# Two halves of one result side by side: where VectorE's list has the first norm's sum in the third quarter of a band

## What is computed

```python
def _arsinh_norm(x, w, b):
    return w * jnp.arcsinh(x) + b
...
    qkv = x @ qkv_w + qkv_b
    q, kk, v = jnp.split(qkv, 3, axis=-1)
...
    scores = jnp.einsum('bijnd,bijmnd->bijnm', q, nb_k)
    attn = jax.nn.softmax(scores, axis=-1)
    out = jnp.einsum('bijnm,bijmnd->bijnd', attn, nb_v).reshape(B, H, W, C)
    return out @ proj_w + proj_b
...
h1 = _arsinh_norm(h, n1_w, n1_b)
h = h + _na2d(h1, qkv_w, qkv_b, proj_w, proj_b)
h2 = _arsinh_norm(h, n2_w, n2_b)
ff = jax.nn.gelu(h2 @ mlp_w1 + mlp_b1, approximate=False) @ mlp_w2 + mlp_b2
return h + ff
```

## Time and profile before

| what | value |
|---|---|
| median of 3 runs | 4478.32 us (4474.22 to 4479.34) |
| the profiled execution's own time | 4478.71 us |
| its span | 4476.9 us |
| busy share: TensorE, VectorE, ScalarE, GpSimd | 91%, 80%, 82%, 79% |
| granted clock of TensorE, share of full speed | 0.97 |
| chain that ended last: TensorE, VectorE, issue, ScalarE | 51%, 23%, 14%, 10% |

### The profile page before, as it was taken

The page is one execution under the profiler, slowest core; times in us unless marked ns, Lnnn a source line. Parts: engine busy times, 40 slices in busy tenths (PEclk is TensorE's granted clock), DMA queues, the critical chain, the costliest instruction groups (busy, mean ns, idle before and its releaser), DMA issues.

```text
span 4476.9 us, 123492 instructions
## 1 busy us (share of the span) xinstructions
PE 4089.1 (91%) x47688; PEld 2566.3 (57%) x47688; DVE 3570.1 (80%) x6174; ACT 3663.0 (82%) x5377; POOL 3539.3 (79%) x4092
## 2 busy tenths in 40 slices
PE   5999999999999999999999999999999999999997
PEld 3555555555555555555555555555555555555553
DVE  5788788888878888887888888788878888887884
ACT  4888888888888888888888888888888888888884
POOL 2788888887888888888878888888888788788885
PEclk8999999999999999999999999999999999999998
DMA  4555555555555555555555555555555555555551
GB/s 121 129 142 134 136 135 138 138 134 137 138 135 134 141 137 132 142 134 138 133 140 138 133 136 139 136 133 142 133 137 135 138 138 133 137 138 136 134 133 55
DMA packets 511560, 598.82 MB, mean 134 GB/s; under 512 B 76798, under 2 KB 409600, under 8 KB 508416
## 3 DMA queue, kind: packets, MB, share of 16 engines
q1 hardware_dynamic: 510976, 590.93, 51.2%
HBM read 197.30 MB, written 135.40 MB: 74 GB/s over the span
## 4 chain that ended last, share of the span: by engine, by line
PE 51%; DVE 23%; issue 14%; ACT 10%; POOL 1%; SPq 1%; DMA 0%; DVEq 0%; POOLq 0%; ACTq 0%
PE ps L369 49%; DVE ln_u L717 4%; DVE y L790 4%; DVE v_nat L771 4%; DVE o_norm L812 3%; DVE ln_u L713 3%; ACT ln_s L920 3%; ACT ln_s L911 3%; ACT ln_s L915 3%; DVE ln_u L710 2%; ACT q_nat L944 2%; PE ps L446 2%; DVE maxima L796 2%; DVE recip L803 1%; POOL g_lo L1098 0%
## 5 line engine op out<-in xcount | busy, mean ns | idle before, releaser
L1072 POOL TENSOR_TENSOR p_lo<-prob,p_hi 100x512 f16<-100x512 f32 x1024 | 1312.7, 1287 | 623.7 <-ACT p_hi L990 623.5
L369 PE MATMUL ps<-b_hi,w_hi 128*128 128x512 f16 x1024 | 435.7, 425 | 288.4 <-DVE y L790 283.3
L989 ACT ACTIVATE prob<-ps 100x512 f32<-100x512 f32 x1024 | 610.2, 596 | 80.2 <-PE ps L369 54.9
L713 DVE TENSOR_TENSOR ln_u<-ln_u,ln_s 128x1024 f32<-128x1024 f32 x256 | 531.0, 2074 | 147.2 <-ACT ln_s L920 143.4
L812 DVE TENSOR_TENSOR o_norm<-ps,recip 64x128 f32<-64x128 f32 x2048 | 591.7, 289 | 49.4
L1098 POOL TENSOR_TENSOR g_lo<-g,g_hi 128x512 f16<-128x512 f32 x512 | 594.9, 1162 | 41.0
L369 PEld LDWEIGHTS ps<-v_win,p_hi 100*128 100x128 f16 x8192 | 474.7, 98 | 261.3 <-DVE o_norm L812 70.7
L990 ACT ACTIVATE p_hi<-ps 100x512 f16<-100x512 f32 x1024 | 613.7, 599 | 0.0
L796 DVE TENSOR_REDUCE maxima<-ps 128x8 bf16<-128x800 f32 x512 | 504.6, 986 | 88.3 <-PE ps L369 84.2
L369 PE MATMUL ps<-v_win,p_hi 100*128 100x65 f16 x8192 | 517.5, 194 | 47.7 <-DVE o_norm L812 26.4
L997 ACT ACTIVATE g<-ps,b 128x512 f32<-128x512 f32 x512 | 344.6, 686 | 254.5 <-PE ps L369 253.6
(11 more groups left out here) (91 smaller groups left out, 10887.7 us busy)
## 6 DMA issues: line engine op xcount, KB each, us to landing
keys<-k_win SPq DMA_DIRECT2D x1536, 100.0 KB, 2.2
v_win<-v_rows SPq DMA_DIRECT2D x1024, 101.6 KB
queries<-q_nat SPq DMA_DIRECT2D x1536, 64.0 KB
v_rows<-v_nat SPq DMA_DIRECT2D x256, 260.0 KB, 5.4
xT<-in_x_dram SPq DMA_DIRECT2D x128, 512.0 KB, 4.3
out_dram<-y SPq DMA_DIRECT2D x256, 256.0 KB, 2.7
queries<-in_query_mask_dram SPq DMA_DIRECT2D x128, 160.0 KB
keys<-in_mlp_w_dram SPq DMA_DIRECT2D x2, 512.0 KB, 7.7
```

What stands on the lines that cost most here:

```text
L369: return pe.matmul(o, a, b, start=start, stop=stop, skip_group_check=True)
L713: v.tensor_tensor(u, u, root, ALU.add).then_inc(s, 1)
L989: act.activation(prob[b][0:NK], ps[0:NK, B_ST + b, :], ACT.Exp, scale=INV * INV).then_inc(prob_ready, 1)
L1072: pool.tensor_tensor(p_lo[b][0:NK], prob[b][0:NK], p_hi[b][0:NK], ALU.subtract).then_inc(p_lo_ready, 1)
```

## The change

In quarter k = 2 of `step` on VectorE, `sum1_(t + 3)` goes from its place in front of `result(t - 2, par, 0)` to behind the second normalisation, and `result(t - 2, par, 1)` comes from behind that normalisation to directly behind `result(t - 2, par, 0)`.

```diff
--- before.py
+++ after.py
@@ -880,10 +880,9 @@
                         sum2_(t - 1)
                     if k == 1 and pre:
                         v_low(t + 2, 0)
-                    if k == 2 and fill:
-                        sum1_(t + 3)
                     if k == 2 and fin:
                         result(t - 2, par, 0)
+                        result(t - 2, par, 1)
 
                     if att:
                         sum_reciprocal(t, 2 * k + 1)
@@ -892,8 +891,8 @@
                         magnitude2(t - 1, old)
                     if k == 1 and pre:
                         v_low(t + 2, 1)
-                    if k == 2 and fin:
-                        result(t - 2, par, 1)
+                    if k == 2 and fill:
+                        sum1_(t + 3)
 
             for t_ in queries:
                 zero(t_[:].rearrange("p n g c q -> p (n g c q)").bitcast(U32), 0)
```

## The result

| | us |
|---|---|
| before, median of 4 runs | 4478.4 (4474.2 to 4479.3) |
| after, median of 4 runs | 4547.4 (4546.9 to 4552.2) |
| ratio after to before | 1.0158, 95% interval 1.0141 to 1.0176 |
| predicted | 4585, range 4525 to 4660, slower with 0.88 |

The change costs 69 us, 1.6%. It is in the direction and inside the range of the forecast, 38 us under its number. The profiled execution of the changed kernel took 4552.2 us with a span of 4550.4 us.

A forecast was written before the change was run, and what follows sets the result against it. TensorE sets the pace outside one 2.29 us gap. Full-clock band 33.33 to 34.60 us, plus 0.40 low clock: mean 35.00 against 34.13, +107 us over 123 bands; 4478.7 + 107 - 1 = 4585 us, range 4525 to 4660.

The forecast's parts named there:

- a sharing of bandwidth: Alternative for VectorE's sum beside GpSimd: it would take 2.04 us again and end at 2011.04, 0.3 us later.
- The three due times: New TensorE starts behind the later logarithm: `weighted` [6] at 2014.10, `mlp_in` 3 ending at 2017.63, `weighted` [7] at 2018.03.
- the 1.27 us reach the next band: TensorE's lateness at `weighted` [7], 1.27 us, was to pass in full through unbroken TensorE work to the next band.
- The low clock: TensorE at 1.2 GHz behind its gap, expected every second band at 0.80 us, so 0.40 us per band.
- the slack behind the lower bound: Slack of `mlp_in` 2 and 3, 0.97 us, hiding part of the low clock's 1.61 us and leaving 0.64 us.
- the rival in which only the low clock stays out: Full-clock band of 34.60 us without TensorE's low clock: +0.47 us a band, 4537 us; chance 0.13.
- the low clock comes in every band: Rival: TensorE's low clock behind the gap in each band, 4734 us unhidden or 4635 at the hidden price; chance 0.18.
- the two did not cancel: Denies the no-change rival: GpSimd avoids the bias pair, `mlp_in` 3 ends last, low clock stays out, 4487 us; chance 0.05.
- (c): Tile [7]: `weighted` [7] waits for the normalisation of [6], starts at 2018.03 instead of 2016.76, 1.27 us late, ending last.
- the gap just closes: Faster rival: TensorE's 2.29 us wait for the result goes, 4099 us, or 4290 for half of it; chance 0.08.

The follow-up runs named there:

- the table of four: VectorE's list before or after the change, each with ScalarE's list unchanged or with o_high and exponentials ahead of the logarithm: before 4478 and 4478 us, after 4547 and 4246.
- the long fill: The changed kernel with one VectorE fill of a 128x1536 scratch tile in front of the sum: 4896.5 us, ratio 1.0929.

## Why the prediction was right, and where it was off

**The gain and its going.** The result is made before TensorE wants it, and the gap in front of `mlp_in` is gone, as predicted. It is there again in front of `weighted` [6]: 2.35 us, predicted 2.4. Shown by the rows, and by the sum moved alone, which has the same time without the earlier result; and that the price is ScalarE's queue, by the runs that cleared it with the sum as late as before.

**The logarithm.** Predicted 1.80 us behind the sum's start (2009.00 to 2010.80), measured 1.83 (2042.13 to 2043.96). The sum takes 1.80 us, predicted 1.77, since it waits for GpSimd's subtraction (2041.69 + 1.16 = 2042.85) to end; the fill in front of it showed that its end hangs on that one and not on its own start. The exclusive lock of the Trainium skill, "SBUF — State Buffer", section "Who interferes with whom", which the prediction weighed against a sharing of bandwidth, is what these traces show: the sum ends 1.08 us behind the subtraction that it met, and the subtraction 1.02 us behind the sum where that was first.

**The three due times.** From `weighted` [5] (2040.12) to `weighted` [7] (2051.16) are 11.04 us; predicted 2018.03 - 2006.97 = 11.06. The wait of `mlp_in` 3 for the gelu is 0.31 us as the row counts it; its first matmul starts 0.48 us later than the usual 0.21 us behind the one before it, against 0.56 predicted; `o_low` stands 1.56 us, predicted 1.6.

**What failed: "the 1.27 us reach the next band".** At full clock the band grew by 34.35 - 33.33 = 1.02 us. From `weighted` [7] to the next `weighted` [5] it is 23.32 us now (2074.48 - 2051.16) where it was 23.54 (2040.30 - 2016.76). I took this stretch for unbroken TensorE work and set its last wait, 0.17 us for the normalisation of [4], aside. That wait ends a way over the second norm's sum, and this sum became shorter too:

```profile
2032.37 2.17 DVE L713 TENSOR_TENSOR ln_u<-ln_u,ln_s 128x1024 f32<-128x1024 f32 x1 [1.09 <-ACT ln_s L920]
...
2037.38 1.53 DVE L717 SCALAR_TENSOR_TENSOR ln_u<-h,ln_s 128x1024 uint32<-128x1024 uint32 x1
...
2039.65 0.59 DVE L812 TENSOR_TENSOR o_norm<-ps,recip 64x128 f32<-64x128 f32 x2
```

In the changed kernel:

```profile
2066.78 1.77 DVE L713 TENSOR_TENSOR ln_u<-ln_u,ln_s 128x1024 f32<-128x1024 f32 x1 [1.09 <-ACT ln_s L919]
...
2071.40 1.70 DVE L717 SCALAR_TENSOR_TENSOR ln_u<-h,ln_s 128x1024 uint32<-128x1024 uint32 x1
...
2073.83 0.59 DVE L812 TENSOR_TENSOR o_norm<-ps,recip 64x128 f32<-64x128 f32 x2
```

The sum starts as far behind `weighted` [7] as before, 15.62 us against 15.61, and VectorE stands still nowhere between it and the normalisation. That ends 7.64 us behind the sum's start instead of 7.87: the sum is 0.40 us shorter and the sign of the second norm 0.17 longer. `weighted` [5] starts 0.06 us behind it in both.

Why the sum is shorter: GpSimd's `g_lo` started 0.08 us in front of it before (2032.29 and 2032.37), and 0.47 us in front of it now:

```profile
2066.31 1.16 POOL L1097 TENSOR_TENSOR g_lo<-g,g_hi 128x512 f16<-128x512 f32 x1
```

TensorE got later and GpSimd less so, so the sum waits 0.40 us less. The prediction had said that GpSimd would be late by less than TensorE, but not asked what that does to the operations of VectorE that wait for GpSimd. 0.25 us x 123 = 31 us is most of the 38 us between forecast and result. The link is read from the rows of one band each; no run tested it by itself.

**The low clock.** Predicted 0.40 us per band in the mean, as 0.80 in every second band. Measured 34.70 - 34.35 = 0.35, as some 1.05 in every third. That the mean came out is luck, for its parts did not: both the share of bands and the price were guesses between bounds (the slack behind the lower bound adds up to 0.96 us, not 0.97). The 0.05 us of difference are 6 of the 38 us. The experiments show how large this term can be: it is 0.80 us a band before, nothing in the steady part where the result alone moved, and some 2.06 us with the gap of 3.48 us.

**The rivals.** By the number alone, 4547 us is nearer to the rival in which only the low clock stays out (4537) than to the forecast. The rows decide against it: the low clock is there in a third of the bands, and the band at full clock is 34.35 us and not 34.60. That the low clock comes in every band fell by the same rows, and the two did not cancel: (c) ended last, as forecast. That the gap just closes was given 0.08; the Trainium skill, "Perfetto Trace Analysis", section "Optimization Strategy", advises to make what the gap waits for start sooner. This rival fell for the reason given, since ScalarE had no slack behind the sum; and the table of four shows when it holds: with the queue cleared, the same change gives 232 us. The advice names the right gap; here what was moved back to close it opened the next one.

## What to carry to other kernels

Where engines work ordered lists, ask of a step that is moved back not who needs its result, but what stands in the list of the engine that waits for it: here the sum's result was not urgent, but a logarithm that waited for it had the exponentials of two tiles behind it. Put what is ready in front of what waits, and only then judge the other list: the same change lost 69 us with one list of ScalarE and gained 232 us with the other. And try the halves of a change alone, since here one half by itself gave 130 us.

## What the runs showed of the hardware that I had not expected

A shorter gap of TensorE was worth more than its length. Each count is of the first 122 steps between results. With a gap of 2.29 us in front of `mlp_in`, the engine was at 1.2 GHz behind 62 of them; with 1.45 us at the same place every step was 33.08 or 33.09 us, and the mean granted clock of the run was 0.992. In front of `weighted` [6], a gap of 2.35 us brought 41 long steps, at some 1.05 us each, and one of 3.48 us had 5.5 us at 1.2 GHz behind it every time, at some 2.06 us each. Of the 349 us of the long fill over the changed kernel, 140 are the later sum (1.14 x 123) and 210 what I put down to the clock, (2.06 - 0.35) x 123.
